# Eight and four heads instead of six and six, and the last residual added by TensorE, in a vision tower on one core

## The reference, cut to what matters

```python
# x: 64 images, 3 x 224 x 224; D = 192, 12 heads of 16, 196 tokens per image
h = patches(x) @ W.T                                # [64, 196, 192]
q, k, v = silu(h @ Wq), silu(h @ Wk), silu(h @ Wv)  # split into 12 heads
energy = (q @ k.T) * decay[head]                    # decay: causal, exp(log_slope * distance)
o = (energy @ v) * sigmoid(h @ Wg1 @ Wg2)
h = layernorm(h + layernorm(o @ Wo, ln_w, ln_b))
xn = rms_norm(h, norm_w)                            # then soft mixture of 64 experts
logits = (l2(slots) * scale) @ l2(xn).T             # [64 slots, 196 tokens] per image
y = softmax_tokens(logits) @ xn
y = gelu(y @ fc1 + fc1b) @ fc2 + fc2b               # fc1, fc2 of each slot: 192 x 768, 768 x 192
out = layernorm(h + softmax_slots(logits).T @ y)
```

## Time and profile before

| | us |
|---|---|
| three runs, median (lowest to highest) | 1272.96 (1271.07 to 1275.09) |
| the profiled execution's own time | 1271.87 |
| its span | 1270.1 |
| busy: TensorE, VectorE, ScalarE, GpSimd | 1176.8, 816.3, 735.9, 572.7 |

### The profile page before, as it was taken

How to read it: one execution, slowest core, us unless ns; L and a number is a source line. 1 busy time by engine, 2 the same in 40 slices (tenths; PEclk the granted TensorE clock), 3 DMA queues, 4 the chain that set the end, 5 groups by cost and what they waited for, 6 DMA issues and landing times.

```text
span 1270.1 us, 34978 instructions
## 1 busy us (share of the span) xinstructions
PE 1176.8 (93%) x12938; PEld 955.7 (75%) x12938; DVE 816.3 (64%) x2114; ACT 735.9 (58%) x1677; POOL 572.7 (45%) x878
## 2 busy tenths in 40 slices
PE   4999999999999999999999999999999999996653
PEld 4888888888888888888888888888887556553432
DVE  4677767677777777776767777777775122221897
ACT  5456667767667677666776766767753211110566
POOL 3355545455545455554545554555543000000664
PEclk8999999999999999999999999999999999999555
DMA  4411211111111111121111111111144699997686
GB/s 144 189 49 53 74 65 54 51 60 51 51 51 51 51 51 51 53 72 64 54 52 59 51 51 51 51 51 51 51 162 175 259 422 423 424 423 239 211 261 187
DMA packets 50653, 158.34 MB, mean 125 GB/s; under 512 B 5354, under 2 KB 31328, under 8 KB 38308
## 3 DMA queue, kind: packets, MB, share of 16 engines
q1 hardware_dynamic: 33016, 145.04, 31.0%
q10 hardware_dynamic: 17600, 12.78, 3.3%
HBM read 132.18 MB, written 25.62 MB: 124 GB/s over the span
## 4 chain that ended last, share of the span: by engine, by line
PE 78%; DVE 16%; issue 2%; ACT 1%; DMA 1%; SPq 1%; DVEq 1%; POOL 0%; ACTq 0%; POOLq 0%
PE ps L945 11%; PE ps L946 10%; PE ps L947 10%; DVE p_sb L801 7%; PE ps L1005 7%; PE ps L1040 6%; PE ps L1219 5%; PE ps L1238 4%; PE ps L1083 3%; PE ps L988 3%; PE ps L989 3%; PE ps L1023 2%; DVE res L914 2%; PE ps L1252 2%; PE ps L1243 2%; DVE st L920 2%
## 5 line engine op out<-in xcount | busy, mean ns | idle before, releaser
L423 POOL TENSOR_TENSOR xl<-x_sb,xh 128x392 fp32r<-128x392 f32 x192 | 189.2, 1017 | 86.1 <-DVE gn L776 77.9
L801 DVE TENSOR_TENSOR p_sb<-ps,dec 98x1176 f32<-98x1176 f32 x128 | 176.9, 1382 | 57.0 <-PE ps L1005 57.0
L1005 PE MATMUL ps<-qm,kT 32*98 32x196 f32 x1536 | 117.0, 343 | 9.6 <-DVE p_sb L801 7.6
L1040 PE MATMUL ps<-p_sb,vpad 98*32 98x98 f32 x3072 | 112.4, 250 | 1.9 <-DVE p_sb L801 1.9
L1040 PEld LDWEIGHTS ps<-p_sb,vpad 98*32 98x32 f32 x3072 | 84.5, 109 | 35.4 <-issue 24.7
L656 ACT ACTIVATE hg<-ps 128x768 f32<-128x768 f32 x32 | 26.0, 811 | 145.9 <-PE ps L1243 145.9
L1005 PEld LDWEIGHTS ps<-qm,kT 32*98 32x98 f32 x1536 | 75.2, 158 | 35.2 <-DVE p_sb L801 23.0
L906 DVE COPY y2st<-ps 128x192 f32<-128x192 f32 x32 | 11.4, 358 | 120.4 <-PE ps L1219 120.4
L1267 PE MATMUL ps<-y2b,cbuf 64*98 64x192 f32 x256 | 49.4, 538 | 41.8 <-POOL y2b L523 41.8
L673 ACT ACTIVATE o_sb<-res,nb,rstd 98x192 f32<-98x192 f32 x128 | 59.6, 536 | 48.6 <-DVE nb L929 47.9
L467 POOL TENSOR_TENSOR invn<-nrm,expo 98x4 f32<-98x4 f32 x32 | 32.7, 1023 | 117.4 <-DVE nrm L786 117.1
(11 more groups left out here) (186 smaller groups left out, 3627.6 us busy)
## 6 DMA issues: line engine op xcount, KB each, us to landing
x_sb<-in_xT SPq DMA_DIRECT2D x32, 1176.0 KB, 5.2
w1v<-in_fc SPq DMA_DIRECT2D x32, 1152.0 KB, 10.0
w2v<-in_fc SPq DMA_DIRECT2D x32, 1152.0 KB, 12.6
h_dram<-h SPq DMA_DIRECT2D x32, 294.0 KB
h2r<-h_dram SPq DMA_DIRECT2D x32, 294.0 KB
out<-o_sb ACTq DMA_DIRECT2D x32, 294.0 KB
comb_dram<-cst SPq DMA_DIRECT2D x32, 98.0 KB, 1.7
cbuf<-comb_dram SPq DMA_DIRECT2D x32, 98.0 KB, 4.0
```

Of the source, the lines that this page charges most:

```text
L423: pool.tensor_tensor(xl[:, k], x_sb[:, k], xh[:, k].bitcast(F32), ALU.subtract)\
L801: dve.tensor_tensor(dst, src, rate.unsqueeze(2).to_broadcast([T, PAIRS, 2, TOK]), ALU.mult)\
L1005: mm = pe.matmul(ps[0:T, SC_AT + r, mt * TOK:(mt + 1) * TOK].rearrange("p (b n) -> p b n", b=2), kT[rows, g, n], qm[rows, g, :, n], start= ...
L1040: mm = pe.matmul(ps[32 * b:32 * b + 32, 5 + g, a * TOK + mt * T:a * TOK + mt * T + T], vpad[:, 2 * a + mt, 32 * (g * HG + h):32 * (g * HG ...
```

## The change

- **Heads.** Groups of eight and four: `kA`, `qA` hold eight heads of both images on 128 partitions (392 columns), `kB`, `qB` the four others, image 0 on partitions 0 to 63 and image 1 on 64 to 127 (196 columns). Attention has three rounds: eight heads of image 0, eight of image 1, four of both. A round has 8 score products (four strips), 98 x 1568 elements in `decay`, 16 value products.
- **Queries.** ScalarE writes `qB` in four pieces of 64 x 196; the separate `qs` is gone, GpSimd makes `qd` from the two halves by an add and a multiply. `zs` is copied ahead of `qB`, and VectorE's part of `zs` waits for `qB` (`q_sb`).
- **v** is projected in two halves (`rows_of_v`): the first ahead of k as before, the second after the first scores and the gate.
- **Output projection.** `ogh`, `ogl` and the two instructions for each are gone; `project_out` multiplies float32 `og` with float32 `wo`: two products on 128 rows and two on 64 rows for each call (x = 0, 1).
- **token_features, logits** use 128 + 64 rows in the same manner.
- **Squares** go to a tile of their own (`sq`) and come later on ScalarE.
- **The first `cbuf` and `h2r` loads** are issued ahead of the second part's weight loads, no more behind them.
- **Passage.** TensorE does 30 products whose result isn't used (`idle_products(6, 30)`), behind the last fc2.
- **Last part.** TensorE starts each bank with an identity product over 384 columns of `h2r`, which puts the residual there, and adds the combine products. `res` is gone: statistics and ScalarE read PSUM. The shift of pair p - 1 is written between the second and third statistics of pair p.

```diff
--- before.py
+++ after.py
...
-        kT = place("kT", [G, 2, PT])
-        qm = place("qm", [G, 2, 2, PT])
+        kA, kB = place("kA", [128, PT]), place("kB", [128, TOK])
+        qA, qB = place("qA", [128, 2, PT]), place("qB", [128, 2, TOK])
...
+            sp.wait_ge(h2_stored, 16 * NP)
+            sp.wait_ge(comb_stored, 16 * NP)
+            for n in range(DEEP):
+                load_comb(n, n)
+                load_h2(n, n)
...
-            sp.wait_ge(h2_stored, 16 * NP)
-            sp.wait_ge(comb_stored, 16 * NP)
-            for n in range(DEEP):
-                load_comb(n, n)
-                load_h2(n, n)
...
-                    for g in range(2):
-                        act.wait_ge(og_sb, 2 * i - 1 + g)
-                        act.activation(ogh[:, g], og[:, g], ACT.Copy).then_inc(ogh_rdy, 1)
                 if d:
...
-                        act.wait_ge(q_mm, 2 * i + g + 1)
-                        act.activation(qm[:, g, 0], ps[0:G, g, 0:PT], ACT.Silu, scale=parity[:, 0:1])
-                        act.activation(qm[:, g, 1], ps[0:G, g, 0:PT], ACT.Silu, scale=parity[:, 1:2])
-                        second = ps[0:G, g, 0:PT].rearrange("p (a c m) -> p a c m", a=2, c=2)[:, :, 1]
-                        act.activation(qs[:, g], second, ACT.Silu).then_inc(q_sb, 1)
+                    act.wait_ge(q_mm, 2 * i + 1)
+                    act.activation(qA[:, 0], ps[:, 0, 0:PT], ACT.Silu, scale=parity[:, 0:1])
+                    act.activation(qA[:, 1], ps[:, 0, 0:PT], ACT.Silu, scale=parity[:, 1:2]).then_inc(q_sb, 1)
+                    act.wait_ge(q_mm, 2 * i + 2)
                     for row in (0, ZT):
-                        act.activation(zs[row:row + RANK, :], ps[G:G + RANK, 1, 0:PT], ACT.Copy).then_inc(zh_rdy, 1)
-                    for g in range(2):
-                        act.wait_ge(v_mm, 2 * i + g + 1)
-                        dst = vpad[:, 2 * g:2 * g + 2].rearrange("p t (j q d) -> p (t j) q d", q=4, d=HD)
-                        src = ps[0:T, V_AT[g], 0:2 * D].rearrange("p (j q d) -> p j q d", q=2, d=HD)
-                        act.activation(dst[:, :, 0:4:3, :], src, ACT.Silu).then_inc(v_sb, 1)
-                    for g in range(2):
-                        act.wait_ge(k_mm, 2 * i + g + 1)
-                        act.activation(kT[:, g], ps[0:G, g, 0:PT], ACT.Silu).then_inc(k_sb, 1)
+                        act.activation(zs[row:row + RANK, :], ps[DB:DB + RANK, 1, 0:PT], ACT.Copy).then_inc(zh_rdy, 1)
+                    for a in range(2):
+                        for b in range(2):
+                            last = act.activation(qB[DB * a:DB * a + DB, b], ps[0:DB, 1, a * TOK:(a + 1) * TOK],
+                                                  ACT.Silu, scale=parity[0:DB, b:b + 1])
+                    last.then_inc(q_sb, 1)
+                    turned_v(i, 0)
...
-                    act.activation(o_sb[:, n, t], res[:, n, t], ACT.Identity,
+                    act.activation(o_sb[:, n, t], ps[0:T, 2 * n + t // 2, (t % 2) * D:(t % 2) * D + D], ACT.Identity,
...
             def decay(i, k):
-                g, a = ORDER[k]
-                if k >= 2:
-                    dve.wait_ge(val_mm, 4 * i + k - 1)
-                dve.wait_ge(sc_mm, 4 * i + k + 1)
-                src = ps[0:T, SC_AT:SC_AT + PAIRS, 0:PT].rearrange("p r (c n) -> p r c n", c=2)
-                dst = p_sb[:, k % 2].rearrange("p c (r n) -> p r c n", r=PAIRS)
-                rate = dec[:, g * HG:(g + 1) * HG].rearrange("p (r b) n -> p r (b n)", b=2)
-                dve.tensor_tensor(dst, src, rate.unsqueeze(2).to_broadcast([T, PAIRS, 2, TOK]), ALU.mult)\
+                if k == 2:
+                    dve.wait_ge(val_mm, 3 * i + 1)
+                dve.wait_ge(sc_mm, 3 * i + k + 1)
+                src = ps[0:T, SC_AT:SC_AT + 4, 0:PT].rearrange("p r (c n) -> p r c n", c=2)
+                dst = p_sb[:, k % 2].rearrange("p c (r n) -> p r c n", r=4)
+                heads = dec[:, 0:HA] if k < 2 else dec[:, HA:HX]
+                rate = heads.rearrange("p (r b) n -> p r (b n)", b=2)
+                dve.tensor_tensor(dst, src, rate.unsqueeze(2).to_broadcast([T, 4, 2, TOK]), ALU.mult)\
                     .then_inc(p_rdy, 1)
...
-                        dve.wait_ge(ogh_rdy, 2 * i - 1 + g)
-                        dve.tensor_tensor(ogl[:, g], og[:, g], ogh[:, g].bitcast(F32), ALU.subtract)\
-                            .then_inc(ogl_rdy, 1)
...
             def out_step(p, n, w):
                 dve.wait_ge(cmb_mm, p + 1)
-                dve.wait_ge(h2r_loaded[n], 16 * w + 16)
-                if not at_start(w):
-                    dve.wait_ge(o_rdy, 4 * (p + 1 - DEEP))
-                dve.tensor_tensor(res[0:T, n].rearrange("p (x t) d -> p x (t d)", x=2),
-                                  ps[0:T, 2 * n:2 * n + 2, 0:2 * D],
-                                  h2r[:, n].rearrange("p (x t) d -> p x (t d)", x=2), ALU.add)\
-                    .then_inc(res_rdy, 1)
-                dve.wait_ge(res_rdy, p + 1)
                 for t in range(4):
-                    dve.bn_stats(st3[:, n, t, :], res[0:T, n, t])
+                    if t == 2 and not (at_start(w) and n == 0):
+                        shift(p - 1, (n - 1) % DEEP)
+                    dve.bn_stats(st3[:, n, t, :], ps[0:T, 2 * n + t // 2, (t % 2) * D:(t % 2) * D + D])
                 dve.drain()
                 for t in range(4):
                     dve.bn_aggr(mv3[:, n, t, :], st3[:, n, t, :]).then_inc(mv3_rdy, 1)
-                if not (at_start(w) and n == 0):
-                    shift(p - 1, (n - 1) % DEEP)
...
+            def project_out(j, x, d_before):
+                pe.wait_ge(og_sb, 2 * j + 2)
+                if x == 1 and d_before:
+                    pe.wait_ge(cb_sb, j - 1)
+                    pe.wait_ge(yT_sb, 2 * j - 2)
+                for a in range(2):
+                    t = 2 * a + x
+                    pe.matmul(ps[0:T, SC_AT + 2 * x + a, 0:D], og[:, t * T:(t + 1) * T], wo[:, 0],
+                              start=True, stop=False)
+                for a in range(2):
+                    rows = slice(DB * a, DB * a + DB)
+                    mm = pe.matmul(ps[0:T, SC_AT + 2 * x + a, 0:D], og[rows, PT + x * T:PT + (x + 1) * T],
...
-                        for b in range(HG // 2):
-                            h = 2 * b + odd
-                            mm = pe.matmul(ps[32 * b:32 * b + 32, 5 + g, a * TOK + mt * T:a * TOK + mt * T + T],
-                                           vpad[:, 2 * a + mt, 32 * (g * HG + h):32 * (g * HG + h) + 32],
-                                           p_sb[:, k % 2, mt, h * T:(h + 1) * T],
-                                           start=(a == 0 and mt == 0 and odd == 0), stop=False)
+                        for r in range(4):
+                            a, h = (k, 2 * r + odd) if k < 2 else (r // 2, HA + 2 * (r % 2) + odd)
+                            at = (a * TOK if k < 2 else 0) + mt * T
+                            mm = pe.matmul(ps[32 * r:32 * r + 32, 6 + k // 2, at:at + T],
+                                           vpad[:, 2 * a + mt, 32 * h:32 * h + 32],
+                                           p_sb[:, k % 2, mt, (2 * r + odd) * T:(2 * r + odd + 1) * T],
+                                           start=(k != 1 and mt == 0 and odd == 0), stop=False)
...
+            def carried(i, g):
+                if g == 0:
+                    pe.wait_ge(s_sb, i + 1)
+                    pe.wait_ge(qd_rdy, 2 * i + 2)
+                for a in range(2):
+                    if g == 0:
+                        mm = pe.matmul(ps[:, 6, a * TOK + T:a * TOK + 2 * T], state[:, a * DA:(a + 1) * DA],
+                                       qd[:, a], start=False, stop=(a == 1))
+                    else:
+                        rows = slice(DB * a, DB * a + DB)
+                        mm = pe.matmul(ps[rows, 7, T:2 * T], state[rows, 2 * DA:2 * DA + DB], qd[rows, 2],
+                                       start=False, stop=True)
                 mm.then_inc(pv_mm, 1)
 
             def slot_inputs_turned(j):
...
-                for t in range(4):
-                    for k in range(2):
-                        mm = pe.matmul(ps[0:T, 7, S * t:S * t + S], tokT[0:G, k, t * T:(t + 1) * T], slT[:, k, :],
-                                       start=(k == 0), stop=(k == 1))
+                pe.wait_ge(tokT_sb, 2 * j + 2)
+                for x in range(2):
+                    at = slice(LG_AT + S * x, LG_AT + S * x + S)
+                    for a in range(2):
+                        t = 2 * a + x
+                        pe.matmul(ps[0:T, 6 + a, at], tokT[:, t * T:(t + 1) * T], slT[:, 0, :], start=True, stop=False)
+                    for a in range(2):
+                        rows = slice(DB * a, DB * a + DB)
...
+                    pe.wait_ge(q_sb, 2 * i + 2)
+                    pe.wait_ge(zl_rdy, i + 1)
+                    project(i, 1, wkh, wkl, k_mm)
```

(21 more changed lines are left out.)

387 lines of the change are left out of this document (201 added, 186 removed).

## The result

| | before | changed |
|---|---|---|
| median (lowest to highest), us | 1272.33 (1271.07 to 1275.09) | 1286.16 (1284.97 to 1287.1) |
| span of the profiled execution | 1270.1 | 1283.2 |
| ratio of the times, 95 % interval | | 1.0108 (1.0088 to 1.0128) |

The forecast was 1257. The kernel became 13.8 us slower; the two spans differ by 13.1 us. Where these lie comes from reading the same four places again.

What follows compares the result with a forecast made beforehand. TensorE's list was taken to bound the first part, a VectorE-GpSimd ring the changed last part. Terms -3 - 2.4 - 2.0 - 4 - 3.5 = -15 us, from 1271.9 to 1257; range 1238 to 1273.

Steps and rivals of the forecast that it cites:

- Output projection, token_features, logits: First part, TensorE's list from embedding to q projection: +0.1, +0.3 and 0 us a pair.
- 0.16 is paid to go in and out: First part: price in us of changing tiling around a tiled group, read from the value products.
- the first rival in its mild form: First part: tiling costs more than 0.16 a group; mild form reaches 1272, 0.3 more gives 1289; rival 12 in 100.
- q to k: First part, q to k projection: ScalarE's chain decides, -0.1 us a pair; the 1.07 us saved becomes waiting.
- First scores to the next pair: First part, rest of a pair: three rounds take 11.3 us instead of 11.83, -0.5; third scores wait 0.4 for decay.
- First and last pairs: First part's ends: three rounds instead of four, -2.4 us; output projection starts at once behind the last round, -2.0.
- Passage: Between second and last part: loads gone from there, last y stored in 2 us, -4 us (bounds 0 and 4.8).
- The queue was still behind: Passage: the last y's store was slow because y's first portion stood behind the cbuf and h2r loads.
- Last part: Last part: 32 pairs at 2.58 instead of 2.66 us, 2.6 us less; with the ends -3.5 us.
- ring of 2.58 us: Last part: VectorE and GpSimd wait on each other in turn, setting 2.58 us a pair although res is gone.
- shift until E + 1.54: Last part: from the means' end E, reciprocal ready at E + 1.38, VectorE's shift done at E + 1.54 us.
- TensorE's step: Last part at 2.4 GHz: two identity products and two tiled pairs take 2.1 us with tiling, under 2.58.

Runs made afterwards that it cites:

- merged: Changed kernel with the products of token_features and logits reordered, two tiled groups less a pair, same products: 1270.99 us, ratio to before 0.9996.
- split: Changed kernel with token_features alternating two transposes and two tiled products, one tiled group more a pair: 1294.62 us, ratio to before 1.0183.
- zl_early: Changed kernel with VectorE's low part of zs waiting only for ScalarE's two zs copies, no longer for qB: 1265.68 us, ratio to before 0.9955.
- loads_back: Changed kernel with the eight cbuf and h2r loads put back behind the second part: 1294.17 us, ratio to before 1.0183.
- bias_after_nb: Changed kernel with GpSimd's sum for y2b of pair p + 4 held until VectorE's shift of pair p is done: 1274.99 us, ratio to before 1.0026.
- shift_last: Changed kernel with VectorE's shift of pair p - 1 put back behind the four means of pair p: 1271.32 us, ratio to before 0.9999.
- no_idle: Changed kernel without the 30 unused products in the passage: 1289.39 us, ratio to before 1.0133.
- res_back: Changed kernel with the whole last part as before (res on VectorE, no identity products, shift behind the means): 1279.13 us, ratio to before 1.0051.

## Why the prediction was wrong, point by point

- **Output projection, token_features, logits** (forecast +0.1, +0.3, 0). Measured 2 x (1.24 - 1.07) = +0.34, 0.97 - 0.62 = +0.35, and 1.53 - 1.35 = +0.18. This is the first step that failed: "0.16 is paid to go in and out". That price came from a long group, the value products. A small group costs 0.24 to 0.31, as merged and split show, and there are five a pair: 5 x 0.12 = 0.6 us. This was the first rival in its mild form; it had 12 in 100. I took the price from the only row at hand, though that row was of a long group. That the measured 1286 lies close to the rival's 1289 is luck: that number stood for 0.3 more a group, and with the 0.12 that were paid, the same working gives about 1274 (29 x 0.6 - 15 = +2); the last part made the rest. The Trainium skill, "TensorEngine Tiling (Array Packing)", section Tiling Modes, has the rule that a change of mode drains TensorE; split agrees that the number of changes, not the work in them, is what is paid: 0.31 us a pair for one more, with the same products.
- **q to k** (forecast -0.1, a wait of about 1.1 us). Measured 6.83 us to the first scores instead of 6.88, wait 1.09: right. The chain qA, `zs`, `qB`, low part in a row is confirmed by zl_early. Right in size, but I booked that microsecond as lost and didn't see that VectorE waited for `q_sb` without need.
- **First scores to the next pair** (-0.5, 11.3 us). Measured 430.14 - 418.74 = 11.40 us instead of 11.83, -0.43; `decay` 1792 ns (forecast 1790). Right, though third scores waited 0.19 us for `decay` and not 0.4.
- **Not forecast**: the rest, 0.17 a pair, lies in the turned hidden rows and embeddings beside these pieces (turned rows 0.48 + 0.72 instead of 0.44 + 0.67).
- **First and last pairs** (-2.4, -2.0). Measured -2.5, and -1.4 for all from the last pair's start on, in which the last pair's own +0.5 lies: right.
- **Passage** (-4, store of the last y in 2 us). Measured -4.7 and 2.6 us; loads_back gives back 5.2. Right in size, and the loads were the cause. "The queue was still behind" is less exact: the store has a queue of its own, ScalarE's, and was longer while the other moved more. The unused products took 6.8 us, not 6.4; they end where the first step begins and don't stand in the way.
- **Last part** (-3.5; ring of 2.58 us). Measured +6.5 and 2.95. The second step that failed is "shift until E + 1.54": it took the shift at its length from the trace before, where it stood beside nothing, and moved it to a place where GpSimd starts its sum 0.06 us ahead of it. Both wait for the end of the same reciprocal, so that they would meet could be read from the order of the lists. bias_after_nb turns the 2.95 into 2.56. The ring itself, which hid what `res` saved, was right. A moved instruction keeps its duration only if its neighbour on the other engine is looked at too.
- **TensorE's step** there, 2.1 us forecast, is 2.29. It didn't bind in the changed kernel, and does in the first half of shift_last's last part. The clock was forecast right at 1.00.

The two terms make the difference: steady pairs 18.3 us (15.3 instead of -3), last part 10 us (6.5 instead of -3.5). The first and last pairs add 0.5 and the passage takes 0.7 off: 1257 + 28 = 1285, the profiled execution's own time (1284.97). The steady pair of 30.01 us is also one of the prediction's signs of being wrong (over 29.9).

## What to carry to other kernels

Count how often TensorE goes between full-width products and tiled ones, and put what is tiled side by side, whatever function it belongs to: here each small group of its own cost 0.24 to 0.31 us, about as much as its products. When a small instruction is moved, look at what GpSimd does at the new place: here a VectorE instruction with two SBUF inputs ended only with GpSimd's sum, at 0.55 us instead of 0.16. And a wait that the sum leaves standing is a place to put work into: half of a projection there, and one semaphore chosen more exactly, brought 33 us, more than all the change was forecast to.

## What the runs showed of the hardware that was not expected

- A VectorE instruction of 98 x 4 elements took 0.55 us instead of 0.13 to 0.16, 28 times in a row, because a GpSimd sum of 0.59 us had started 0.06 us before it.
- A group of two to four tiled products between full-width ones costs 0.24 to 0.31 us for being there, 1.5 to 1.9 times what the long value groups show (0.16). Why a long group pays less stays open.
- The last part's own steps, with full-width identity products and no gap at the lower clock, brought TensorE from 0.50 to 1.00 without unused products (no_idle). In res_back it began at 1.00 and fell to 0.50 though no gap was longer than 2.87 us, and it stayed there with gaps of 0.9 to 1.4 us in every step.
- Eight loads ahead of the last y's way to memory and back cost 5 us, although the 96 KB store was issued on another queue: it took 7.7 us beside 230 GB/s and 2.6 beside 83. Some 3 more went because the clock fell while TensorE waited.
